# A tile of expert results laid out the other way round in a mixture-of-experts stage

## The reference

```
y1 = ln(x + mha(x)) * ln1_g + ln1_b
gates = softmax(y1 @ wg);  idx = argmax(gates)          # one of 8 experts
h = disp @ w1[e] + b1[e];  y = h @ w2[e] + b2[e]        # no nonlinearity between
out = gate_val * y of the chosen expert, or 0 if the expert is over its capacity
y2 = ln(y1 + out) * ln2_g + ln2_b
```

## Time and profile before

| | |
|---|---|
| time, median of 3 executions | 4637.02 us (4636.9 to 4659.84) |
| the profiled execution, its own time | 4655.05 us |
| its span from the first to the last instruction | 4653.3 us |
| mean granted TensorE clock of that execution | 0.897 of full speed |
| busy over the span: PE, DVE, ACT, POOL | 83%, 67%, 37%, 34% |
| expert parts in ACT (L2094), 512 instructions | 143.1 us busy |
| bias parts in ACT (L2130), 16 instructions | 9.2 us busy |
| sums in DVE (L2374), 64 instructions | 136.6 us busy |

### The profile page before, as it was taken

One profiled execution on the slowest core, in us unless ns is written; L12 is line 12 of the kernel. 1 busy time (PEld: TensorE's weight loads), 2 busy tenths in 40 slices (PEclk: granted clock), 3 DMA queues, 4 the chain that ended last, 5 costly groups with the idle time before them and its releaser, 6 DMA issues. The chain is left out here.

```text
span 4653.3 us, 163745 instructions
## 1 busy us (share of the span) xinstructions
PE 3861.4 (83%) x66245; PEld 2812.4 (60%) x66245; DVE 3117.4 (67%) x6104; ACT 1733.8 (37%) x3495; POOL 1595.7 (34%) x2519
## 2 busy tenths in 40 slices
PE   6999999866648998989988989989899998588860
PEld 4666666533326776767776767767677766455530
DVE  3777777747746676767666766767677654288858
ACT  1222222224423343444443433434444432277750
POOL 1333333311004454444444444544444443100001
PEclk6998999988858999999999999999999987699975
DMA  0222222136522222222222222222222221111105
GB/s 25 44 47 46 55 56 49 42 84 155 158 65 49 42 56 41 47 51 48 50 47 49 48 49 40 57 42 47 51 48 49 49 47 26 55 27 28 28 18 149
DMA packets 695281, 251.77 MB, mean 54 GB/s; under 512 B 529368, under 2 KB 660128, under 8 KB 694176
## 3 DMA queue, kind: packets, MB, share of 16 engines
q1 hardware_dynamic: 694560, 241.62, 23.7%
HBM read 154.63 MB, written 86.79 MB: 52 GB/s over the span
## 5 line engine op out<-in xcount | busy, mean ns | idle before, releaser
L1373 POOL TENSOR_TENSOR d_f<-d_ms,d_mhalf 128x16 f32<-128x16 f32 x64 | 239.5, 3742 | 965.1 <-DVE d_ms L1807 965.1
L1567 PE MATMUL d_pa<-d_wv,d_hs 128*128 128x512 f32 x1024 | 517.6, 652 | 0.9 <-DVE d_qk L1778 0.4
L1761 DVE SCALAR_TENSOR_TENSOR d_acc<-d_pa,d_cq,d_acc 128x512 f32<-128x512 f32 x576 | 431.7, 750 | 95.2 <-ACT d_acc L1406 80.3
L1383 POOL TENSOR_TENSOR d_prod<-d_ablk,d_tblk 128x15 f32<-128x15 f32 (+7 forms) x960 | 342.5, 357 | 218.5 <-DMA d_ablk<-a_blocks 147.9
L1387 POOL TENSOR_TENSOR d_tblk<-d_tblk,d_prod 128x28 f32<-128x28 f32 (+7 forms) x896 | 336.4, 375 | 70.8 <-POOL d_prod L1383 0.2
L1567 PEld LDWEIGHTS d_pa<-d_wv,d_hs 128*128 128x128 f32 x1024 | 219.5, 215 | 232.1 <-issue 220.2
L1542 PE MATMUL d_pa<-d_hq,d_wqk 128*128 128x259 f32 x768 | 255.4, 462 | 81.4 <-DVE d_acc L1761 58.0
L1406 ACT ACTIVATE d_acc<-d_pa,d_cq 128x512 f32<-128x512 f32 x192 | 131.9, 687 | 420.8 <-PE d_pa L1542 418.0
L262 POOL TENSOR_TENSOR a_act<-a_act,a_cws 128x512 f32<-128x512 f32 x128 | 166.8, 1316 | 310.2 <-DMA a_cws<-cw_rows 165.3
L1580 PEld LDWEIGHTS d_pb<-d_of_head,d_sqT 128*128 128x128 f32 x2048 | 246.2, 196 | 39.2 <-issue 39.0
L1370 POOL TENSOR_TENSOR d_nr<-d_n,d_half_power 128x16 f32<-128x16 f32 x64 | 188.0, 2938 | 193.8 <-DVE d_n L1846 179.8
(11 more groups left out here) (371 smaller groups left out, 9418.3 us busy)
## 6 DMA issues: line engine op xcount, KB each, us to landing
a_cws<-cw_rows SPq DMA_DIRECT2D x32, 1024.0 KB, 10.5
decays<-g_dec SPq DMA_DIRECT2D x16, 2048.0 KB, 7.3
d_dd<-decays SPq DMA_DIRECT2D x64, 512.0 KB, 4.3
d_hs<-h_t SPq DMA_DIRECT2D x512, 32.0 KB, 2.2
t_blocks<-d_tblk SPq DMA_DIRECT2D x128, 128.0 KB, 1.7
a_blocks<-d_at SPq DMA_DIRECT2D x512, 16.0 KB, 1.9
d_ablk<-a_blocks SPq DMA_DIRECT2D x64, 128.0 KB, 2.1
d_tt<-t_blocks SPq DMA_DIRECT2D x512, 16.0 KB
```

The costliest lines, as they stand in the source:

```text
L1373: pool.tensor_tensor(f[:, :], ms[:, :], mhalf[:, :], ALU.pow).then_inc(sem("f_ready"), 1)
L1383: link(pool.tensor_tensor(prod[:, 0:n, 0:s + 1], ablk[:, s, s + 1:SB].unsqueeze(2).to_broadcast([P, n, s + 1]), tblk[:, 0, s, 0:s + 1].uns ...
L1567: last = pe.matmul(pa[:, B + m, :], hs[:, u % 2, t, :], wv[:, t, cols(m)], start=(t == 0), stop=(t == TAPS - 1))
L1761: last = dve.scalar_tensor_tensor(out=own, in0=raw(e)[:, :, t:t + QT], scalar=cq[:, t, col:col + 1], in1=own, op0=ALU.mult, op1=ALU.add)
```

## The change

The last two dimensions of `part` change places. The nine words of one feature (eight experts and the bias) now lie side by side, so DVE's sum reads 1152 consecutive words a column. ACT's writes, of the expert parts and of the bias, now go in steps of nine words (36 bytes). No instruction is added, removed or moved, no wait changes, and the tile has the same size.

```diff
-        part = sb("part", [P, NC, NE + 1, D])
+        part = sb("part", [P, NC, D, NE + 1])
...
-                        last = act.activation(part[:, c, e, :], xp[:, (e - e0) * D:(e - e0 + 1) * D], ACT.Identity,
+                        last = act.activation(part[:, c, :, e], xp[:, (e - e0) * D:(e - e0 + 1) * D], ACT.Identity,
                                               scale=rt[:, m % 2, 1, c, e:e + 1])
...
-                    act.activation(part[:, :, NE, :], tiles(turned), ACT.Copy).then_inc(sem("bias_taken"), 1)
+                    act.activation(part[:, :, :, NE], tiles(turned), ACT.Copy).then_inc(sem("bias_taken"), 1)
...
-                    dve.tensor_reduce(moe[:, c, :], part[:, c, :, :].rearrange("p e d -> p d e"), AX_X, ALU.add)\
+                    dve.tensor_reduce(moe[:, c, :], part[:, c, :, :], AX_X, ALU.add)\
                        .then_inc(sem("reduced"), 1)
```

## The result

The changed kernel takes 4694.59 us (median of 4 executions, 4684.76 to 4699.74) against 4636.96 for the kernel before on the same chip: a ratio of 1.0114, 95% interval [1.0074, 1.0155], so about 53 us slower. Forecast were 4685 and "slower". The profiled execution took 4691.75 us, its span is 4690.0 and its mean granted clock 0.887 (0.897 before). The number came out; the way to it did not, and that is what most of the following is about.

A forecast was written before the change was run, and what follows sets the result against it. ACT alone was taken to bound the softmax stretch, PE and ACT in turn the rest; 42 us (14 iterations) + 6.9 (iterations 16 and 17) - 0.8 (last sum) = +48 us, put on the median of 4637.02: 4685 us, range 4634 to 4738.

The forecast's parts named there:

- What bounds the stage: Attention stage: ACT alone paces the softmax stretch, PE and ACT alternate elsewhere; only the last DVE sum counts, -0.8 us.
- The sum: DVE's 64 sums: each falls from 2134 to 1355 ns, 50 us of DVE time over the stage.
- The price of a stepped word on ACT: ACT's writes of parts and bias: 1.73 ns a stepped word, taken from a DVE read, 0.90 more than consecutive.
- A weighing 0.46 us longer on the path, five times in the stretch with the bias, 3.0 us an iteration: ACT's groups of four part writes and bias copy: stepped words paid in full, 42 us over 14 softmax iterations.
- Rival 1: ACT's stepped writes drain in its own gaps; only bias and last part before a hand-over pay: +8 us, 4645; chance 0.12.
- Iterations 16 and 17, +6.9 us: Last two iterations: 15 groups of ACT's part writes alternate with PE and pay 0.46 us each in full.
- The clock: PE's granted clock falls in half of 14 iterations as ACT's longer stretch idles PE: +33 us, 4718; chance 0.16.
- rival 3: PE's clock follows: ACT's longer stretch leaves PE idle, so its granted clock falls; +33 us, 4718; chance 0.16.

The follow-up runs named there:

- run 5: Kernel before, old layout, with DVE's sums taking five of the nine parts only (experts 0 to 3 left out); ratio 1.0000 to the kernel before.
- run 10: Third layout: two neighbouring features side by side, then the next expert, so ACT writes runs of two words; ratio 0.9992 to the kernel before.
- run 3: Changed kernel plus seven unused PE products of 128 x 256 an iteration, to keep PE busy; ratio 0.9981 to the kernel before.
- run 1: Kernel before plus a second ACT copy of the bias into a tile nobody reads, nothing stepped; ratio 1.0013 to the kernel before.
- run 6: Changed kernel with the bias copied by DVE instead of ACT, just before the first sum; ratio 1.0055 to the kernel before.
- run 2: Changed kernel with stepped expert parts, but the bias in its own tile in consecutive words, added by DVE; ratio 1.0086 to the kernel before.
- run 8: Changed kernel with ACT's writes in steps of 24 words (96 bytes) instead of nine; 4722.88 us in a single execution.
- run 12: Kernel before, consecutive writes, with a one-word ACT copy behind each four parts that gives PE the signal; ratio 1.0083 to the kernel before.
- run 9: Kernel before, old layout, with the bias copied by DVE instead of ACT and four parts left out of the sums; ratio 0.9961 to the kernel before.
- run 4: Kernel before plus seven unused PE products of 128 x 256 an iteration, to keep PE busy; ratio 0.9962 to the kernel before.

## Why the prediction was right, and where it was wrong

- *What bounds the stage*: right. ACT sets the pace in the stretch of the softmaxes, PE and ACT in turn in the rest, and no sum is waited for but the last (runs 5 and 10).
- *The sum*: right, 1353 ns for 1355.
- *The price of a stepped word on ACT*: forecast 1.73 ns, measured 1.69 (from the bias). The row of a DVE read was a good guide to an ACT write of the same tile.
- *A weighing 0.46 us longer on the path, five times in the stretch with the bias, 3.0 us an iteration*: wrong, and it was 42 of the 48 us. This is the step that failed. Four parts hold ACT 0.02 us longer, an iteration is 0.55 us longer. The step took price times words and added it to ACT's time, though the row beside it had shown that a part of 0.11 us of words takes 0.25 us. Rival 1, given 0.12, said just this, with 0.5 us an iteration.
- *Iterations 16 and 17, +6.9 us*: not seen; the program takes 0.4 us less from the last L2417 on. The granted clock there was higher after than before (0.74 for 0.70 up to the last sum), so a cost of a few microseconds could be hidden.
- *The clock*: a rival with 0.16, priced at +33 us. It is the main term, 43.5 us by the account, and run 3 shows it. Its reason, a longer stretch, was not it either: run 1 has that and loses 6 us, run 6 has a shorter one and loses 25. What the runs with long falls share is the later hand-over of each half (2, 6, 8, 12 and the changed kernel); those without a later hand-over (1, 5, 9, 10) have no fall of more than 11 us.

So that 48 forecast and 53 measured agree is luck: rival 1 and rival 3 came true together, 7 us of one and 43.5 of the other in the profiled executions, and the prediction had no case in which both hold.

Open is why the clock falls where it does. That it falls in two of three iterations here, in one of two in run 2 and in none but one before was read off, not explained. The later hand-over is shown for the long falls, 29.5 us of the loss. The falls of 10 us, another 18.7, come without it too (one before and in run 5, two in run 1), and why the changed kernel has four is not shown. How often a fall begins may also hang on how the length of an iteration lies in time, the timing theory of run 9: runs 2 and 12 have the same 28.62 us, and no run separates the two. Runs 6 and 9 also differ in DVE's copy and sum, so the pair alone does not settle the hand-over; run 12 changes nothing else but 0.2 us of ACT time.

## What to carry to other kernels

Price an access pattern on the interval from one instruction's start to the next one's, not on its duration, and then ask who waits for its end: a write that is free for its own engine can still be late for another. Where TensorE idles in short gaps beside a busier engine, read the granted clock per iteration before and after: here 0.06 to 0.14 us at a hand-over became 7 to 8 us in four to six of 13 iterations. When two sides want opposite layouts, try runs of two words before choosing a side.

## What the runs showed of the hardware

- A sum that steps by two words (8 bytes) is as fast as a consecutive one, 1353 ns for 1152 words (run 10), while steps of 512 bytes took 2134. The Trainium skill (SBUF — State Buffer, section "Specifications (TRN2)") gives lines of 16 bytes that want two hits each for full bandwidth; the trace agrees with that for steps of 8 bytes. The rule of the Trainium skill that the prediction quotes, the full rate only for runs of two neighbouring words, is too narrow for this read, whose words stand alone.
- ACT pays for steps when it writes: 1.69 ns a word at 36 bytes (changed kernel) and 2.39 at 96 (run 8), where consecutive ones take 0.83. Runs of two words with hops of 72 bytes cost almost nothing (369 ns a part for 356, run 10).
- A fall of the clock is nearly free where PE has time to spare (some 3.5 us at the lower level in an iteration of 29.29 us, for 28.9 without, run 1).
- Products that compute nothing made the kernel before 0.4% faster, 0.2 to 0.6 by the interval (run 4).
